# A two-layer graph network on one core: attribute sums, parts of x and the lower parts of z go to GpSimd, one-hots go back to VectorE

## What is computed

```python
def _mp_layer(x, src, dst, edge_attr, W, b):      # adds a self loop of weight 0 to every node
    msg = concatenate([x[dst2], x[src2], ea2], axis=1) @ W + b
    return relu(segment_sum(msg, dst2, num_segments=n))
h   = relu(_mp_layer(x, src, dst, edge_weight1, W1, b1))      # 64 -> 128
out = _mp_layer(h, src, dst, edge_weight1, W2, b2)            # 128 -> 64
result = layernorm(x + log_softmax(out, axis=1))
```

## Time and profile before

| | |
|---|---|
| median of 3 runs | 193.68 us |
| the profiled execution | 193.38 us |
| its span, first to last instruction | 191.3 us |
| busy: PE, DVE, ACT, POOL | 173.1, 161.4, 114.1, 98.6 us |
| mean granted TensorE clock | 0.979 |

### The profile page before, as it was taken

How to read it: one execution, slowest core, us unless ns; L and a number is a source line. 1 busy time by engine, 2 the same in 40 slices (tenths; PEclk the granted TensorE clock), 3 DMA queues, 4 the chain that set the end, 5 groups by cost and what they waited for, 6 DMA issues and landing times.

```text
span 191.3 us, 5193 instructions
## 1 busy us (share of the span) xinstructions
PE 173.1 (90%) x2050; PEld 157.6 (82%) x2051; DVE 161.4 (84%) x407; ACT 114.1 (60%) x197; POOL 98.6 (52%) x192
## 2 busy tenths in 40 slices
PE   7686587999999999999999999999999999999940
PEld 2133376998899987999999999999999999999930
DVE  0989999999999999999979979729429969888773
ACT  2526897888888989999989989863311102012201
POOL 6388504799889988988999989500000000000000
PEclk9969999999999999999999999999999999999995
DMA  1336200000000000000000000000000010200010
GB/s 45 103 90 146 65 11 2 6 1 4 1 6 1 4 1 4 2 4 1 3 0 3 2 3 0 3 0 5 0 3 2 16 27 0 44 13 17 20 25 20
DMA packets 9032, 3.35 MB, mean 18 GB/s; under 512 B 8240, under 2 KB 8557, under 8 KB 9007
## 3 DMA queue, kind: packets, MB, share of 16 engines
q1 hardware_dynamic: 8207, 2.08, 5.3%
q0 software_dynamic: 800, 0.93, 2.2%
HBM read 2.18 MB, written 0.81 MB: 16 GB/s over the span
## 4 chain that ended last, share of the span: by engine, by line
PE 64%; DVE 26%; DMA 5%; issue 3%; ACT 1%; DVEq 0%
PE pset L1126 18%; PE acc L1079 18%; DVE oh L569 16%; PE pset L1057 11%; PE acc L1126 9%; PE epb L1109 3%; PE epb L1120 3%; DMA adj<-in_edges,adj 3%; DMA adj<-in_dst 2%; DVE adj L556 1%; PE epb L1097 1%; DVE u L601 1%; DVE adj L581 1%; DVE x L586 1%; PE epb L1111 1%
## 5 line engine op out<-in xcount | busy, mean ns | idle before, releaser
L441 POOL TENSOR_SCALAR oh<-iota,keys 128x125 bf16<-128x125 bf16 x132 | 78.2, 615 | 14.9 <-PE pset L1057 14.3
L909 ACT ACTIVATE adj<-pset 125x1000 bf16<-125x1000 f32 (+1 forms) x79 | 78.4, 996 | 10.0 <-PE pset L1057 7.2
L569 DVE TENSOR_TENSOR oh<-iota_bank,keys 128x1764 bf16<-128x1764 bf16 (+4 forms) x81 | 83.1, 1051 | 0.4 <-PE pset L1057 0.3
L1079 PE MATMUL acc<-x,adj 125*125 125x195 bf16 x625 | 65.4, 248 | 0.3 <-DVE x L586 0.3
L1079 PEld LDWEIGHTS acc<-x,adj 125*125 125x125 bf16 x625 | 54.7, 136 | 0.9 <-issue 0.5
L1057 PE MATMUL pset<-oh 128*128 128x125 bf16 x625 | 47.3, 218 | 6.8 <-DVE oh L569 4.8
L1057 PEld LDWEIGHTS pset<-oh 128*128 128x128 bf16 x625 | 38.6, 97 | 10.4 <-ACT adj L909 6.1
L1126 PE MATMUL pset<-z,adj 125*125 125x192 bf16 x425 | 36.8, 246 | 0.0
L1126 PEld LDWEIGHTS pset<-z,adj 125*125 125x125 bf16 x425 | 35.5, 136 | 0.1
L988 ACT ACTIVATE x<-x 125x192 f32<-125x192 f32 (+2 forms) x6 | 2.6, 427 | 32.4 <-DVE x L737 32.4
L1126 PE MATMUL acc<-z,adj 125*125 125x192 bf16 x200 | 17.5, 246 | 0.0
(11 more groups left out here) (125 smaller groups left out, 150.5 us busy)
## 6 DMA issues: line engine op xcount, KB each, us to landing
x_nat<-in_x_tiles SPq DMA_DIRECT2D x1, 406.2 KB
x_nat<-in_x_tiles SPq DMA_DIRECT2D x1, 375.0 KB
out<-x SPq DMA_DIRECT2D x2, 187.5 KB
out<-x SPq DMA_DIRECT2D x3, 93.8 KB
adj<-in_dst SPq DMA_DIRECT2D x1, 208.5 KB
bw<-adj SPq DMA_DIRECT2D x9, 1.0 KB
out<-x SPq DMA_DIRECT2D x1, 125.0 KB
adj<-in_edges,adj POOLq DMA_INDIRECT x5, 4.9
```

The costliest lines, as they stand in the source:

```text
L441: ins = gp.tensor_scalar(oh[k % 3][:, OWN, side, 0:Q], iota1[:, 0:Q], keys[:, place(k * SET + OWN), side, 0:1], None, ALU.is_equal)
L569: ins = dve.tensor_tensor(out=oh[k % 3][:, at_w:at_w + m, :, 0:2 * PAIRS].rearrange("p w t (q e) -> p (w t) q e", e=2), in0=iota_p.unsquee ...
L909: ins = act.activation(bands[c][0:Q, :, at_w:at_w + n * WD].rearrange("p h (w e) -> p h w e", e=WD), rows[:, 0:n, 0:WD * G].rearrange("p w ...
L1079: ins = pe.matmul(acc[g % 2][0:Q, 0:XW], block_of_adj(g, h), x3[:, h, 0:XW], start=(h == 0), stop=(h == G - 1))
```

## The change

It does these things:

- GpSimd makes no one-hots any more: `onehots(k)` on VectorE makes all 8 windows of every set.
- The attribute sums go from VectorE to GpSimd. VectorE took one instruction per column, 25 in all; GpSimd takes five compares, one product over 5 x 128 elements and seven halving adds for each batch j, 65 in all, each depending on the one before from the product on. They are written into GpSimd's order among the splits of sums: sums 0 and 1, split 0, sums 2, z 0, split 1, sums 3, z 1, split 2, sums 4 and so on.
- For the first six epilogues GpSimd makes the middle and the low part of z (`low_of_z`), in place of `cast_middle` on ScalarE and `z_low` on VectorE.
- GpSimd makes both `low_of_x` and the second `rest_of_x`, between its gathers.
- The transfer of the second part of x is asked for after the third offset, ahead of the weights, and ScalarE casts it ahead of `evacuate(0)`. The gathers' order changes too.
- q_f of the first batch is made on ScalarE, the bias casts come later, and batches 3 and 4 of `distances` come at set 24 and 30 instead of 28 and 34.

```diff
-DIST_BLOCK = {1: 2, 2: 14, 3: 28, 4: 34}
-SUM_SET = {0: 16, 1: 24, 2: 31, 3: 37, 4: 43}
+DIST_BLOCK = {1: 2, 2: 14, 3: 24, 4: 30}
+POOL_Z = 6
...
# GpSimd
             gather_edges(0)
+            gather_edges(1)
             gather_attrs(0)
-            gather_edges(1)
-            gather_attrs(1)
-            for j in range(2, J):
-                gather_edges(j)
-            for j in range(2, J):
+            low_of_x(0, 0, XA)
+            rest_of_x(1, XA, G)
+            gather_edges(2)
+            low_of_x(1, XA, G)
+            gather_edges(3)
+            gather_edges(4)
+            for j in range(1, J):
                 gather_attrs(j)
...
+            def attr_sums(j):
+                gp.wait_ge(attrs_in[j], 16)
...
+                for r in range(WD):
+                    gp.tensor_scalar(se_mask[:, r, :], d_f[:, j, :], float(r), None, ALU.is_equal).then_inc(mask_chain, 1)
+                done = j * (WD + 7) + WD
+                gp.wait_ge(mask_chain, done)
+                gp.tensor_tensor(se_mask, se_mask, attrs[:, j:j + 1, :].broadcast_to([Q, WD, SLOTS]), ALU.mult).then_inc(mask_chain, 1)
+                for n in (64, 32, 16, 8, 4, 2):
+                    done += 1
+                    gp.wait_ge(mask_chain, done)
+                    gp.tensor_tensor(se_mask[:, :, 0:n], se_mask[:, :, 0:n], se_mask[:, :, n:2 * n], ALU.add).then_inc(mask_chain, 1)
+                gp.wait_ge(mask_chain, done + 1)
+                gp.tensor_tensor(se_w[:, j, :], se_mask[:, :, 0], se_mask[:, :, 1], ALU.add).then_inc(se_ready, 1)
+
+            def low_of_z(i):
+                a, b = EPILOGUES[i]
+                gp.wait_ge(rest_ready, i + 1)
+                gp.tensor_copy(z3[:, a:b, C:2 * C], u[i % 2][:, 0:b - a, 0:C]).then_inc(pool_mid, 1)
+                gp.wait_ge(pool_mid, i + 1)
+                gp.tensor_tensor(z3[:, a:b, 2 * C:3 * C], u[i % 2][:, 0:b - a, 0:C], z3[:, a:b, C:2 * C], ALU.subtract)\
+                  .then_inc(z3_ready, 1)
...
# VectorE
-            def attr_sums(j, r0, r1):
...
-                n = OWN if shared(k) else set_size(k)
+                n = set_size(k)
...
-            bias_rest(0)
...
-            low_of_x(0, 0, XA)
             onehots(4)
-            rest_of_x(1, XA, G)
...
# ScalarE
-            cast_bias(0)
             cast_x(0, 0, XA)
+            act.wait_ge(pairs_in[0], 16)
+            act.wait_ge(loops_ready, 2)
+            act.activation(q_f[:, 0, :], pairs[:, 0, 0::2], ACT.Copy, scale=1.0 / Q, bias=-float(Q // 2) / Q).then_inc(q0_ready, 1)
...
+            cast_x(1, XA, G)
             evacuate(0)
             evacuate(1)
-            cast_x(1, XA, G)
+            cast_middle_x(1, XA, G)
...
-                    if b == turn_block(i) + 6:
+                    if i >= POOL_Z and b == turn_block(i) + 6:
                         cast_middle(i)
...
# SyncE
             sp.dma_start(x_nat[:, 0:XA, :], x_tiles[:, 0:XA, :]).then_inc(xnat_in[0], 16)
+            sp.wait_ge(off_ready, 3)
+            sp.dma_start(x_nat[:, XA:G, :], x_tiles[:, XA:G, :]).then_inc(xnat_in[1], 16)
...
-            sp.wait_ge(pairs_in[0], 16)
-            sp.dma_start(x_nat[:, XA:G, :], x_tiles[:, XA:G, :]).then_inc(xnat_in[1], 16)
```

More of the change, by code:

```diff
@@ L431, in split_sums @@
                 gp.tensor_copy(s2, r[:, :, 1:2].broadcast_to(wide)).then_inc(se_parts, 1)
-            def last_onehot(k):
-                gp.wait_ge(built, k - 2)
-                for j in range(J):
-                    if k * SET <= j * Q < (k + 1) * SET or k == SHARED_FROM and j * Q < k * SET <= (j + 1) * Q:
-                        gp.wait_ge(keys_ready, j + 1)
-                for side in range(2):
-                    ins = gp.tensor_scalar(oh[k % 3][:, OWN, side, 0:Q], iota1[:, 0:Q],
-                                           keys[:, place(k * SET + OWN), side, 0:1], None, ALU.is_equal)
-                ins.then_inc(last_ready, 1)
@@ L445, in _ @@
-            for k in range(NSETS):
-                for j in range(J):
-                    if k == SPLIT_BLOCK[j]:
-                        split_sums(j)
-                if shared(k):
-                    last_onehot(k)
+            def attr_sums(j):
+                gp.wait_ge(attrs_in[j], 16)
+                if j:
+                    gp.wait_ge(dist_ready, j)
+                    gp.wait_ge(se_ready, j)
+                else:
+                    gp.wait_ge(key_ready, 1)
+                for r in range(WD):
[9 more added lines that the diff above has]
+                gp.tensor_tensor(se_w[:, j, :], se_mask[:, :, 0], se_mask[:, :, 1], ALU.add).then_inc(se_ready, 1)
@@ new lines, in low_of_z @@
+            def low_of_z(i):
[5 more added lines that the diff above has]
+                  .then_inc(z3_ready, 1)
+            attr_sums(0)
+            attr_sums(1)
+            split_sums(0)
@@ L453, in _ @@
+            attr_sums(2)
+            low_of_z(0)
+            split_sums(1)
+            attr_sums(3)
+            low_of_z(1)
+            split_sums(2)
+            attr_sums(4)
+            low_of_z(2)
+            split_sums(3)
+            low_of_z(3)
+            split_sums(4)
+            for i in range(4, POOL_Z):
+                low_of_z(i)
             gp.wait_ge(flag_ready, 1)
@@ L534, in key_distances @@
                 dve.wait_ge(loops_ready, 2)
-                dve.tensor_scalar(d_f[:, j, :], pairs[:, j, 1::2], thr_neg[:, j:j + 1], None, ALU.add)
-                link(dve.tensor_scalar(q_f[:, j, :], pairs[:, j, 0::2], -float(Q // 2), 1.0 / Q, ALU.add, ALU.mult))
+                link(dve.tensor_scalar(d_f[:, j, :], pairs[:, j, 1::2], thr_neg[:, j:j + 1], None, ALU.add))
+                dve.wait_ge(q0_ready, 1)
             def key_tiles(j):
@@ L548, in key_sums @@
                                          op0=ALU.is_le, op1=ALU.mult).then_inc(key_ready, 1)
-            def attr_sums(j, r0, r1):
-                dve.wait_ge(attrs_in[j], 16)
-                if j:
-                    dve.wait_ge(dist_ready, j)
-                for r in range(r0, r1):
-                    dve.scalar_tensor_tensor(out=se_junk[:, j * WD + r, :], in0=d_f[:, j, :], scalar=float(r),
-                                             in1=attrs[:, j, :], op0=ALU.is_equal, op1=ALU.mult,
-                                             accum_out=se_w[:, j, r:r + 1]).then_inc(se_ready, 1)
             def onehots(k):
-                n = OWN if shared(k) else set_size(k)
+                n = set_size(k)
                 if k >= 3:
@@ L663, in _ @@
                         key_sums(j)
-                for j in range(J):
-                    if 0 <= k - SUM_SET[j] < WD:
-                        attr_sums(j, k - SUM_SET[j], k - SUM_SET[j] + 1)
                 for g in range(G):
@@ L877, in copy_keys @@
                     act.wait_ge(oh_ready, done + 1)
-                    act.wait_ge(last_ready, done + 1 - SHARED_FROM)
                 mine = slice(j % 2 * Q, (j % 2 + 1) * Q)
@@ L1054, in build @@
                 for i in range(set_size(k)):
-                    if shared(k) and i == OWN:
-                        pe.wait_ge(last_ready, k - SHARED_FROM + 1)
                     ins = pe.matmul(pset[k % 2][:, i // 4, i % 4 * 128:i % 4 * 128 + WD * G],
```

43 lines of the change are left out of this document (21 added, 22 removed).

## The result

| | before | after |
|---|---|---|
| median, 11 runs each | 193.68 us | 192.07 us (191.29 to 193.15) |
| the profiled execution, and its span | 193.38, 191.3 us | 191.90, 190.1 us |
| busy DVE, ACT, POOL | 161.4, 114.1, 98.6 us | 161.1, 112.8, 65.2 us |
| mean granted TensorE clock | 0.979 | 0.983 |

What follows compares the result with a forecast made beforehand. VectorE was taken to set the pace up to about set 23, TensorE behind it. The terms -2.3 + 0.1 - 0.9 = -3.1 on 193.38 gave 190.3, with 0.3 for the median 190.6 us, range 188.8 to 195.0.

Steps and rivals of the forecast that it cites:

- What bounds the kernel: VectorE sets the pace up to about set 23, so work taken off it there moves the end; TensorE behind that.
- 2.76 in the sum: VectorE ahead of set 25's end: three operations on x gone, -0.90 - 0.93 - 0.93 = -2.76 us.
- GpSimd's prices: GpSimd's operations on x and attribute sums: 1.9 ns an element, 1.7 and 1.8 us for x, 7.65 us a batch.
- Rival 1: GpSimd late at the turns of b = 21 and 29, gain shrunk, attribute batch 9.0 us: about 193 us; chance 0.13.
- rival 2: GpSimd at 3.4 ns an element, attribute batch 9.6 us, split 0 5.0 late for b = 21: about 197 us; chance 0.15.
- The front sum of -2.3: VectorE's work from first one-hot to set 25's end changes by -2.3 us, moving the turn at b = 21 to 50.2.
- rival 3: GpSimd's long reads lengthen six VectorE instructions before the turn by 0.2 to 0.5 us each: 192 to 193.5; chance 0.15.
- The +0.1 for split 0: At the turn at b = 21: sums 0, behind SyncE's nine bias rows, in place at 50.0, just ahead of 50.2; 0.1 us counted.
- one of the prediction's own signs: The prediction is wrong if TensorE's turn at b = 21 waits for `stats`.
- The -0.9 between b = 21 and 35: Between these turns VectorE goes from level with TensorE to 0.8 ahead; 0.9 of the 1.4 us lost is taken back.
- one low z at about 0.3 us: VectorE over sets 26 to 38 before the change: one low z counted within its 18.4 us.
- the stated range: Whole kernel's median: 188.8 to 195.0 us, leaving out most of rival 2 and a little below.

Runs made afterwards that it cites:

- experiment 7: The kernel before with only the change in x (operations on GpSimd, gathers' order, transfer, ScalarE's early casts): 191.31 us, ratio 0.9874.
- experiment 4: The changed kernel with the three operations on x back on VectorE and ScalarE's casts of its second part back in their old places: 194.13 us, ratio 1.0036.
- experiment 8: The kernel of experiment 3 with GpSimd's five compares of each attribute batch made twice, values unchanged: 194.66 us, ratio 1.0061.
- experiment 3: The changed kernel with bias casts behind b = 3, 6, 8 instead of 2, 8, 12, and the second bias rest behind set 12: 190.83 us, ratio 0.9878.
- experiment 1: The changed kernel with the second rest of the bias behind set 12 instead of 14, its cast behind b = 6: 191.29 us, ratio 0.9875.
- experiment 9: The changed kernel with GpSimd's product over 640 elements cut into five instructions of 128: 191.03 us, ratio 0.9873.
- Experiment 2: The changed kernel with SyncE sending the sums of batch 0 ahead of the nine bias rows instead of behind them: 191.57 us, ratio 0.9904.
- Experiment 5: The changed kernel with the middle and low parts of z back on ScalarE and VectorE for all epilogues: 193.54 us, ratio 0.9996.
- experiment 6: The changed kernel with the attribute sums back on VectorE, one-hots and z left as changed: 193.39 us, ratio 0.9984.
- experiment 11: The kernel of experiment 3 (changed kernel with bias casts early) measured once more: 190.74 us, ratio 0.9855.
- experiment 12: The kernel of experiment 3 with GpSimd's product also cut into five pieces, as in experiment 9: 190.99 us, ratio 0.9884.

## Why the prediction was half right, step by step

**What bounds the kernel** held. Taking three operations on x off VectorE gave 2.3 us by itself (experiment 7) and about 2 in the changed kernel (experiment 4, where a shorter meeting of the bias hides part of it), for 2.76 in the sum.

**GpSimd's prices** held. The operations on x took 1.55 and 1.76 us (1.7 and 1.8 predicted), an attribute batch 7.7 (7.65), and sums 0 ended at 39.2 (39.4). Inside it the product was a little dearer (1.56 for 1.4) and a compare cheaper (0.54 for 0.6). From the product and the add of 5 elements, (1.559 - 0.20) / 635 = 2.14 ns an element, for the 1.9 that the prediction took. The prediction's estimate from the Trainium skill (GPSIMD Engine Reference, § 3.1), 4497 ns for 2048 elements, came to 2.2; the trace agrees. Rival 1 fell, and so did rival 2, whose mechanism experiment 8 shows at a price of 10.3 us.

**The front sum of -2.3 is the step that failed.** It put at nothing what GpSimd's instructions cost VectorE's, which the prediction had only as rival 3, at a chance of 0.15, and it did not ask whether ScalarE keeps up. In after, VectorE ends set 25 at 50.65 (49.46 + 1.19), and TensorE's turn comes 1.25 us behind that set where nothing else holds it, as in experiment 3 (49.41 and 50.66). In before it ended set 25 at 51.27 (50.20 + 1.07). So VectorE gained 0.6 and not 2.3. The 1.7 that are missing:
- +1.27: the rest of the bias met the long product (1.56 for 0.29).
- +0.59: the key tiles of batch 1 waited for ScalarE, 0.29, and took 0.51 for 0.21, the 0.30 being another meeting, with an indirect transfer. The prediction brought VectorE to these tiles over 3 us sooner and did not ask whether `distances(1)` was there; in experiment 3, where it stands ahead of the bias cast, VectorE waits for nothing, and comes to the tile early enough in GpSimd's transfer to be spared the 0.30 too.
- -0.17: the first one-hot came 0.47 sooner (14.91 for 15.38), and not 0.3.

The sum, 1.69, is what is missing. Experiment 3 ends set 25 at 49.41, 1.86 sooner than before. The 0.44 that it lacks to 2.3 is again such a meeting, 0.62 at 42.69, less 0.26 by which its first one-hot (14.82) came sooner than forecast. So the widths, the columns and x came as summed, to 0.1.

Rival 3 had the right cause and the wrong form, and the measured 192.07 is the lower end of its 192 to 193.5. It spread 0.2 to 0.5 us over six instructions. What came was one of them at 1.27, the others in the stretch being near their own length, and one with a single input at 0.30. For the 1.27 experiments 1, 3 and 9 show it, each by another edit: an earlier place or shorter instructions on GpSimd bring it down to 0.29 or 0.47. The Trainium skill (SBUF — State Buffer, § Who interferes with whom) calls this an exclusive lock on a pair of ports that the two engines share, and the trace agrees: the instruction ends 0.14 us after GpSimd's.

**The +0.1 for split 0** should have been +0.7, and one of the prediction's own signs came: the turn waited for `stats`. The links by themselves held: from the sending of the sums to the last part took 6.0 us (46.39 to 52.40), the nine rows 5.64. But the links hung on set 16, behind which the last bias cast waits. VectorE ended that at 38.6 (predicted 36.4), mostly since the 1.27 and the 0.59 lay ahead of it. So the same loss came in twice, through VectorE and, a little longer, through SyncE. With 0.2 us between the two, the prediction should have asked what a late VectorE does to both. Experiment 2 takes it away and gives 0.8 at the turn.

**The -0.9 between b = 21 and 35** came out at 0.90, for a reason that was only partly the one given. The sum was made of widths and columns, and put one low z at about 0.3 us. Experiment 5 shows that without z on GpSimd the whole 0.9 is gone (21.15 us), because `z_low` is back on VectorE and the attribute sums lengthen it and `scale_x` by 0.6 each. Moving the sums without z wins nothing in this stretch, and moving z without the sums (experiment 6, 21.13 us) wins nothing either. The prediction gave z 0.3, and it was worth 1.1 (0.9 to 1.5 by the ratios).

**Behind b = 35** another 0.4 us came, for which the prediction had nothing. What it was the runs don't tell. From b = 35 to 78 after takes 55.23 us, before 55.61, experiment 5 55.43 and experiment 6 56.13: so it hangs on VectorE's load too.

**What was luck.** The median lies within the stated range because that was drawn wide enough for rivals 1 and 3, not because the front came out. The 0.4 us behind b = 35, for which the prediction had no term, made up for a part of what was missing, and that is luck.

**Open:** after was measured at 0.9916 and at 0.9950, with intervals that just miss each other, and the difference lies outside the span: there are 2.0 us around it in before, in every series beside an experiment, and in the first series of after, 2.5 in the second, 2.2 to 2.4 in experiments 1 to 4 and 11, 2.0 to 2.1 in 5 to 9 and 12. No run says why. So medians that differ by less than 0.5 us are not settled, where spans and turns are steadier. The front's account above rests on profiles, one execution each, or two for after and experiment 3. L577's 0.30 us beside an indirect transfer is read from rows and no run changed it alone.

## What to carry to other kernels

When GpSimd gets vector work, lay its long instructions against VectorE's program in time and look for the instructions that fall into them, those with two inputs in SBUF above all: the price is what is left of GpSimd's instruction, up to its whole length, and small shifts decide whether it is paid. Put VectorE's such instructions elsewhere, or cut GpSimd's into pieces. If a queue (here nine bias rows on SyncE) hangs on the same loop as the wait that it feeds, a loss in the loop comes out at both, so slack of a few tenths is no slack. And price each part of a bundle by itself: the smallest part of this one, alone in the kernel before, won more than the whole.

## What the runs showed of the hardware

- A VectorE instruction with two fp32 inputs in SBUF took 1.56 us for 0.29 over a GpSimd instruction of 1.55. One with a single input and a scalar (L577) took 0.83 us for 0.21 over the same kind. It is not only the long product: an add of 0.87 us held one up to 0.81 us (experiment 9). One-hots, which read PSUM and SBUF, were untouched: in after, three sets run from 41.24 to 44.66 in 3.42 us, over all of the second product (42.06 to 43.61), the same as before.
- GpSimd's indirect transfers count too. In eight profiles (after in both series, experiments 1, 2, 5, 6, 9 and 12) L577 of batch 1 started 0.58 to 0.75 us into such an instruction of 1.21 us, took 0.48 to 0.65 us and ended 0.02 to 0.04 us after it. In experiments 3, 8 and 11 it started 0.28 to 0.56 us into one and took its own 0.21 or 0.22.
- TensorE's clock is granted at half (1.2 for 2.4 GHz) in stretches that lie elsewhere in each execution. Most have one early, as before (9.1 to 12.5) and after (9.7 to 13.1), ahead of the first one-hot. Experiment 1 had a second at 22.05 to 25.46, experiment 4 one at 24.2 to 27.6, experiments 2 and 11 none ahead of 184. TensorE was busy 2.14 of the 4.05 us ahead of it in experiment 1, and 2.04 in after over the same stretch, where the clock stayed up. So the profile does not show why it fell. Where it falls inside the bound part it costs one to two us, which is about the spread within one kernel's runs (190.38 to 192.51 in experiment 1).
